# Split layer-norm statistics, a later GpSimd start, and store waits moved to the next use of the buffer

## What is computed

```
x = x + gcn(layernorm(x))            # 512 -> 128, aggregate over edges, 128 -> 512
x = x + alu(layernorm(x))            # small 3-layer net; adds only into columns 128..160
x = x + gnn3(layernorm(x))           # three 512x512 layers, each aggregated over edges
x = x + fff(layernorm(x))            # 16 experts, one per token, 512 -> 2048 -> 512
```

## Time and profile before

| | |
|---|---|
| median of 3 runs | 576.83 us |
| profiled execution | 578.86 us |
| its span | 577.1 us |
| TensorE matmul busy | 526.0 us (91%) |
| VectorE / ScalarE / GpSimd busy | 188.4 / 143.6 / 73.1 us |
| bytes moved by DMA | 145.84 MB, mean 253 GB/s |
| chain that ended last | PE 68%, DMA 16%, DVE 8%, issue 3% |

### The profile page before, as it was taken

The page is one execution under the profiler, slowest core; times in us unless marked ns, Lnnn a source line. Parts: engine busy times, 40 slices in busy tenths (PEclk is TensorE's granted clock), DMA queues, the critical chain, the costliest instruction groups (busy, mean ns, idle before and its releaser), DMA issues.

```text
span 577.1 us, 10036 instructions
## 1 busy us (share of the span) xinstructions
PE 526.0 (91%) x3215; PEld 286.8 (50%) x3215; DVE 188.4 (33%) x566; ACT 143.6 (25%) x504; POOL 73.1 (13%) x99
## 2 busy tenths in 40 slices
PE   1969999989999999999999599999999999978884
PEld 1536667544457466445455245555544364434332
DVE  5998999644410110256730100111111011100110
ACT  1547666112102011003122112222222042202211
POOL 4000000090000000000002222211211212122011
PEclk9979999979999999999999799999999999999998
DMA  6159930001120010027799999999999999999980
GB/s 128 14 174 429 429 133 19 18 1 53 39 73 2 0 73 0 7 86 229 288 389 418 413 396 424 420 424 423 422 423 419 419 430 412 421 416 433 420 371 21
DMA packets 26513, 145.84 MB, mean 253 GB/s; under 512 B 10479, under 2 KB 12729, under 8 KB 16882
## 3 DMA queue, kind: packets, MB, share of 16 engines
q1 hardware_dynamic: 23282, 142.92, 61.4%
q0 software_dynamic: 3200, 2.50, 2.1%
HBM read 142.38 MB, written 4.72 MB: 255 GB/s over the span
## 4 chain that ended last, share of the span: by engine, by line
PE 68%; DMA 16%; DVE 8%; issue 3%; ACT 2%; DVEq 1%; ACTq 1%; POOL 0%; POOLq 0%; SPq 0%
PE P L1168 14%; PE P L1082 13%; DMA w<-in_L_ffn_W 12%; PE P L955 9%; PE P L965 7%; PE P L789 6%; PE P L974 4%; DMA XT<-normed_rows,C 2%; PE P L1133 2%; DMA out<-XT,C 2%; DVE stats L1317 2%; DVE H L1292 1%; PE P L790 1%; PE P L1146 1%; PE P L869 1%
## 5 line engine op out<-in xcount | busy, mean ns | idle before, releaser
L1168 PE MATMUL P<-w,FB 128*64 128x256 f32 x1024 | 115.9, 383 | 2.2 <-DMA w<-in_L_ffn_W 2.2
L1082 PE MATMUL P<-w,H 128*64 128x512 f32 x448 | 100.0, 595 | 9.3 <-DMA w<-in_L_ffn_W 8.8
L1168 PEld LDWEIGHTS P<-w,FB 128*64 128x64 f32 x1024 | 72.1, 138 | 40.6 <-issue 6.6
L718 ACT ACTIVATE FB<-P,FB 128x64 f32<-128x64 f32 x256 | 54.4, 361 | 121.8 <-PE P L1133 121.8
L1575 DVE COPY H<-P 128x512 f32<-128x512 f32 x30 | 20.7, 692 | 195.5 <-PE P L1082 195.0
L789 PE MATMUL P<-H 125*126 125x500 bf16 x176 | 59.0, 414 | 8.1 <-DVE H L1292 4.7
L1082 PEld LDWEIGHTS P<-w,H 128*64 128x64 f32 x448 | 32.1, 137 | 68.7 <-issue 59.3
L1292 DVE TENSOR_SCALAR H<-iota,small 125x626 bf16<-125x626 f16 x176 | 56.6, 382 | 8.7 <-issue 6.9
L619 ACT ACTIVATE H<-G,small 125x126 bf16<-125x126 f16 x132 | 44.2, 392 | 35.3 <-PE P L790 21.8
L955 PE MATMUL P<-G,XT 128*125 128x512 f32 x120 | 52.0, 592 | 0.0
L965 PE MATMUL P<-C,H 125*128 125x313 f32 (+1 forms) x160 | 42.4, 425 | 0.0
(11 more groups left out here) (315 smaller groups left out, 441.8 us busy)
## 6 DMA issues: line engine op xcount, KB each, us to landing
w<-in_L_ffn_W SPq DMA_DIRECT2D x53, 2048.0 KB, 24.8
w<-in_L_ffn_W SPq DMA_DIRECT2D x14, 1024.0 KB, 9.6
G<-in_L_gnn_W SPq DMA_DIRECT2D x3, 1024.0 KB, 5.3
G<-in_L_ffn_W SPq DMA_DIRECT2D x2, 1024.0 KB, 8.3
C<-in_L_ffn_W SPq DMA_DIRECT2D x2, 1024.0 KB, 9.4
xs<-in_L_ffn_W SPq DMA_DIRECT2D x2, 1024.0 KB, 10.2
xn<-in_L_ffn_W SPq DMA_DIRECT2D x2, 1024.0 KB, 10.3
xs<-in_x SPq DMA_DIRECT2D x1, 1120.0 KB
```

What stands on the lines that cost most here:

```text
L718: g = nc.scalar.activation(hT[:, m, :], P[:, 3 + rd, c * SA:(c + 1) * SA], ACT.Gelu, bias=bT[b][:, m:m + 1])
L1082: mm = nc.tensor.matmul(P[g * SA:(g + 1) * SA, h, :], xT[b][:, k, :], w1a[k][:, h, g], start=(k == 0), stop=(k == KD - 1))
L1168: mm = nc.tensor.matmul(P[g * SA:(g + 1) * SA, 7, 0:256], hT[:, m, :], w2_sb[b][:, m, g * 256:(g + 1) * 256], start=False, stop=(m == MH - 1))
```

## The change

Statistics: `bn_stats` of columns 162 to 511 (`CHANGED` = 162) is done while layer 2 of the four-case network runs, into the second half of a new statistics tile `stats2`; after the additions only columns 0 to 161 are left, and `bn_aggr` joins the two parts. To free VectorE, both halves of layer 2's output are now copied by ScalarE. GpSimd waits for `s_feat` beside `s_ahead` before it starts. One `keep_warm` matmul is added ahead of the wait for `s_fTc`, and one is taken from the seven ahead of the norm. Stores: the scatter of tile i waits for the scatter of tile i - 2 just ahead of its own row numbers, and `s_yfree` is raised there; the first pass of the loop is written out, as it has nothing to wait for.

```diff
--- before.py
+++ after.py
@@ -54,6 +54,7 @@
 NF = 5
 RESULT = 100
 FCOLS = 108
+CHANGED = 162
 
 NE, HID = 16, 2048
 MH = HID // 128
@@ -155,6 +156,8 @@
         win_tail = G[:, 1024 + CASES * GE:1024 + CASES * (GE + GT)].rearrange("p (c o) -> p c o", c=CASES)
         fT = G[:, 0:N_NODES]
         y3T = H[:, 2 * N_NODES:3 * N_NODES]
+
+        stats2 = H[:, 2000:2000 + NCH * 12].rearrange("p (c s v) -> p c s v", c=NCH, s=2)
 
 
         feat = FB[0:NC, 0:NCH * GT].rearrange("p (c f) -> p c f", c=NCH)
@@ -500,6 +503,7 @@
             nc.gpsimd.memset(feat, 0.0).then_inc(s_fz, 1)
 
             pool.wait_ge(s_ahead, 1)
+            pool.wait_ge(s_feat, 1)
             for c in range(NCH):
                 nc.gpsimd.tensor_scalar(xn[0:NC, c, FCOLS:DIM], xs[0:NC, c, FCOLS:DIM], mv[0:NC, c, 0:1], rstd[0:NC, c:c + 1],
                                         ALU.subtract, ALU.mult).then_inc(s_ln, 1)
@@ -508,7 +512,7 @@
 
             pool.wait_ge(s_gh, NCH * 3)
             nc.gpsimd.memset(b2_rows, 0.0).then_inc(s_b2z, 1)
-            pool.sem_inc(s_yfree, 2)
+
             def hold(sem, value):
 
                 pool.wait_ge(sem, value)
@@ -525,8 +529,12 @@
                                              in_offset=bass.IndirectOffsetOnAxis(ap=row_in, axis=0),
                                              bounds_check=2 * N_NODES - 1, oob_is_err=False).then_inc(s_xr, 16)
 
-            def scatter(i, b, count):
-
+            def scatter(p, b, count):
+
+                i = 2 * p + b
+                if not (isinstance(p, int) and p == 0):
+                    hold(s_yst[b], 16 * p)
+                pool.sem_inc(s_yfree, 1)
                 pick(row_out[b], 0, i, count)
                 hold(s_ycp, i + 2)
                 nc.gpsimd.indirect_dma_start(out=out.rearrange("t (g n) -> (t g) n", g=2),
@@ -555,16 +563,15 @@
                 i = 2 * p + b
                 hold(s_xT, i + 2)
                 gather(i + 2, 2 * i + 3)
-                scatter(i, b, 2 * i + 4)
+                scatter(p, b, 2 * i + 4)
                 if isinstance(p, int) and i == LARGE:
                     pool.wait_ge(s_ycpB, 1)
                     nc.gpsimd.indirect_dma_start(out=out.rearrange("t (g n) -> (t g) n", g=4),
                                                  out_offset=bass.IndirectOffsetOnAxis(ap=row_outB, axis=0), in_=y_sbB, in_offset=None,
                                                  bounds_check=4 * N_NODES - 1, oob_is_err=False, compute_op=ALU.add).then_inc(s_ystB, 16)
-                hold(s_yst[b], 16 * p + 16)
-                pool.sem_inc(s_yfree, 1)
-
-            with pool.Fori(0, LARGE // 2) as p:
+            for b in range(2):
+                move_rows(0, b)
+            with pool.Fori(1, LARGE // 2) as p:
                 for b in range(2):
                     move_rows(p, b)
             for b in range(2):
@@ -573,7 +580,7 @@
                 for b in range(2):
                     move_rows(p, b)
             for b in range(2):
-                scatter(2 * last + b, b, 4 * last + 3 + b)
+                scatter(last, b, 4 * last + 3 + b)
             for b in range(2):
                 hold(s_yst[b], 16 * last + 16)
             pool.wait_ge(s_ystB, 16)
@@ -675,8 +682,9 @@
                 nc.scalar.activation(ffn_features(layer, t)[:, a:b], P[:, g % 8, 0:b - a], ACT.Relu,
                                      bias=(bf_c[:, t:t + 1] if layer else 0.0)).then_inc(s_fa, 1)
 
-            act.wait_ge(s_y3, 2)
-            nc.scalar.activation(y3T[:, HALF:N_NODES], P[:, 5, 0:N_NODES - HALF], ACT.Identity, bias=b3_c[:, 0:1]).then_inc(s_y3c, 1)
+            for h, (a, b) in enumerate(HALVES):
+                act.wait_ge(s_y3, h + 1)
+                nc.scalar.activation(y3T[:, a:b], P[:, 4 + h, 0:b - a], ACT.Identity, bias=b3_c[:, 0:1]).then_inc(s_y3c, 1)
             sqrt_var()
             copy_transposed()
 
@@ -883,6 +891,7 @@
                     t = nc.tensor.matmul(P[g * GT:(g + 1) * GT, c // 4, (c % 4) * NC:(c % 4 + 1) * NC], feat[:, c, :],
                                          ident[0:NC, 0:NC], start=True, stop=True)
             t.then_inc(s_fT, 1)
+            keep_warm(1, C[0:NC, 0, 0:DIM])
             pe.wait_ge(s_fTc, 1)
             pe.wait_ge(s_win, 16 * 20)
             pe.wait_ge(s_wint, 1)
@@ -938,7 +947,7 @@
             t.then_inc(s_y3, 1)
 
 
-            keep_warm(7, C[0:NC, 0, 0:DIM])
+            keep_warm(6, C[0:NC, 0, 0:DIM])
             ln_no[0] += 1
             transpose_norm()
 
@@ -1307,17 +1316,17 @@
 
             batch_no = [0]
 
-            def norm(chunk_ready=None, batches=ALL_CHUNKS, ahead=0):
+            def norm(chunk_ready=None, batches=ALL_CHUNKS, ahead=0, halves=False):
 
 
                 for first, end in batches:
                     for c in range(first, end):
                         if chunk_ready:
                             chunk_ready(c)
-                        last = nc.vector.bn_stats(stats[0:NC, c, :], xs[0:NC, c, :])
+                        last = nc.vector.bn_stats(stats2[0:NC, c, 0, :] if halves else stats[0:NC, c, :], xs[0:NC, c, 0:CHANGED if halves else DIM])
                     link(last)
                     for c in range(first, end):
-                        last = nc.vector.bn_aggr(mv[0:NC, c, :], stats[0:NC, c, :])
+                        last = nc.vector.bn_aggr(mv[0:NC, c, :], stats2[0:NC, c].rearrange("p s v -> p (s v)") if halves else stats[0:NC, c, :])
                     link(last)
                     ts(rstd[0:NC, first:end], mv[0:NC, first:end, 1], EPS, None, ALU.add).then_inc(s_var, 1)
                     batch_no[0] += 1
@@ -1387,8 +1396,9 @@
 
             ya, ys, ysel = sv(460, NCH, 4), sv(480, NCH, 4), sv(500, NCH, 4)
             res, oh, car = sv(520, NCH, 2), sv(540, NCH * 2, 16), sv(700, NCH)
-            dve.wait_ge(s_y3, 1)
-            ts(y3T[:, 0:HALF], P[:, 4, 0:HALF], b3_c[:, 0:1], None, ALU.add).then_inc(s_y3c, 1)
+            dve.wait_ge(s_xsum, 1)
+            for c in range(NCH):
+                nc.vector.bn_stats(stats2[0:NC, c, 1, :], xs[0:NC, c, CHANGED:DIM])
             dve.wait_ge(s_y3, 3)
             y3 = P[0:NC, 6, 0:2 * CASES * NCH].rearrange("p (c n) -> p c n", c=NCH)
             tt(ya[0:NC], y3[:, :, 0:4], madd[0:NC, :].unsqueeze(2).to_broadcast([NC, NCH, 4]), ALU.mult)
@@ -1404,10 +1414,9 @@
                     res[0:NC].rearrange("p c s -> p (c s)").unsqueeze(2).to_broadcast([NC, NCH * 2, 16]), ALU.is_equal))
             link(tt(oh[0:NC].rearrange("p (c s) n -> p c (s n)", s=2), oh[0:NC].rearrange("p (c s) n -> p c (s n)", s=2),
                     act2[0:NC, :].unsqueeze(2).to_broadcast([NC, NCH, 32]), ALU.mult))
-            dve.wait_ge(s_xsum, 1)
             tt(xs[0:NC, :, 128:160], xs[0:NC, :, 128:160], oh[0:NC].rearrange("p (c s) n -> p c (s n)", s=2), ALU.add)
             link(tt(xs[0:NC, :, 160:161], xs[0:NC, :, 160:161], car[0:NC, :].unsqueeze(2), ALU.add))
-            norm()
+            norm(halves=True)
 
 
             with dve.Fori(0, 3) as l:
```

## The result

The changed kernel takes 571.49 us (median of six runs, 570.94 to 572.00) against 576.09 for the kernel before in the same comparison (573.65 to 578.91); 4.6 us by the medians and 4.4 by the ratio, 0.9923 (0.9902 to 0.9943). The forecast was 571.0.

The account below looks back on a forecast made before the run. The saturated weight stream was taken as the bound, with gains ahead of it counting in full: 0.65 + 3.1 + 1.7 + 0.8 = 6.25 us, 0.5 less for the median, so 576.83 - 5.8 = 571.0; whole range 567.5 to 574.4.

Parts of the forecast that it names:

- The bound: Expert stage from 330 us on: the saturated weight stream, about 421 GB/s, sets the time, not TensorE.
- a sign that I had named: Expert stage: TensorE's waits on weights grow by about 7 us, those of L1082 several us above 8.8.
- Another sign: Everything ahead of the graph layers: the prediction is wrong if the granted clock is 0.50 anywhere there.
- GpSimd at `s_feat`: Four-case network, ahead of the features: two 20-column VectorE operations drop to 0.17 us each, 0.65 us gained.
- Statistics: Norm behind the four-case network: 162 of 512 columns stay on the path, the rest is hidden, 1.7 us gained.
- `keep_warm` and the clock: Four-case network, layer 0 and the first layer 1 group: the filler keeps the clock up, 3.1 us gained.
- Stores: Expert stage, tile 2: the 6.2 us wait for gathered rows goes, but only 0.8 us is won.
- the thin place: Weight stream over 330 to 342 us: 384 instead of 421 GB/s, priced at 1.05 us.
- (b): Expert stage: TensorE is the bound, so the stall is paid out in full, 7 instead of 0.8, 565; chance 0.06.
- (c): Norm: the hidden statistics aren't hidden, VectorE's 2.4 us stay on the path, 573.4; chance 0.06.
- (d): Weight stream, 330 to 556 us: it loses rate and the kernel is slower, 581 at 403 GB/s; chance 0.05.
- rival (a): Four-case network: clock falls anyway, or median run before never had the low stretch; 3.15 us remain, 573.7; chance 0.15.

Follow-up runs that it names:

- h1: Kernel before with half of the bytes in most expert weight loads, old store waits: 555.24 us, ratio 0.9634.
- s4: Kernel before with only the waits for the stores moved to the buffers' next use: 574.54 us, ratio 0.9979.
- g1: Changed kernel with the gather of tile 3's rows issued ahead of tile 0's scatter: 571.73 us, ratio 0.9926 to the kernel before.
- c0: Changed kernel without the nine keep-warm matmuls ahead of the feature transposes and the one ahead of layer 0: 575.02 us, against 571.68 for the changed kernel beside it.
- s1: Kernel before with only one more keep-warm matmul ahead of the wait for the copied features: 574.96 us, ratio 0.9991.
- l1: Changed kernel without the one keep-warm matmul ahead of the wait for the copied features: 571.43 us, ratio 0.9919 to the kernel before.
- l2: Changed kernel with the waits for the stores as in the kernel before: 571.79 us, ratio 0.9919 to the kernel before.
- s3: Kernel before with the split statistics alone, ScalarE copying both output halves and six keep-warm matmuls instead of seven: 573.12 us, ratio 0.9960.
- a1: The changed kernel measured again, unaltered, on another chip: 571.68 us, ratio 0.9916 to the kernel before.

## Why the prediction came out as it did

- **The bound.** Right: half of the bytes take 21.5 us away (h1), the rate stays at 421 to 422 over 360 to 500 in every trace with all the bytes, and a stall taken out comes back as waiting (s4) or as nothing in the time (g1). But a sign that I had named failed. The waits on weights were to grow by about 7 us, those of L1082 "several us above 8.8"; in the trace of after they are 11.2 against 11.0, and L1091's are 6.0. The stall of 2.5 us that was left, and TensorE's stretches at 1.2 GHz, used up the room. Only s4 and g1, where neither is there, show 16.5 to 16.7. Another sign was worded too widely: the clock is at 1.2 GHz from 31.6 to 38.4 us in the trace of after, but so it is somewhere between 31 and 41 us in every other, before too, far ahead of the change.
- **GpSimd at `s_feat`, 0.65 us.** 0.62 between warm-up and transposes in every trace that has it.
- **Statistics, 1.7 us.** 1.76, in every trace that has it. The hidden part, 350 columns, cost 2.22 us for the 2.4 I worked out and had 1.84 us to spare for 1.5.
- **`keep_warm` and the clock, 3.1 us.** The price was right: 3.2 us between the profiles of before and after from the transposes to the network's result, and 3.0 in c0's trace behind the transposes. Its parts were off a little: layer 0 lost 2.42 us, not 2.54 (I had taken its start and its end from two views), and the first group of layer 1 0.8, not 0.55. That the filler buys it for the median run was the step that failed. I read one profile as the program, with a discount of 0.5 us; it should have been the whole 3.1. That profile, 578.86, was above all six timed runs but one. The filler itself bought nothing that could be measured (s1, l1).
- **Stores, 0.8 us.** Right in mechanism, under-sized: 1.8 us by the traces, some 1.1 of it the thin place I had priced at 1.05 (363 to 392 GB/s over 330 to 342 in the traces with the old waits, 422 to 430 with the new). The median of s4 says 1.3, that of l2 only 0.1 to 0.4. The gather was late by 2.5 us with a scatter just ahead of it, which cost nothing (g1).
- **The sum.** 0.62 + 1.76 + 1.8 = 4.2 us, against 4.6 and 5.1 between the medians of two comparisons (4.4 and 4.8 by the ratios). What is over may be the time that the kernel before takes longer in runs of lower clock, as in s3's median; that isn't shown. From the median of six runs the terms give 576.09 - 4.2 = 571.9. I came to 571.0 with a clock term that is mostly absent, stores that were 1.0 too small, and a median of before (576.83) that was 0.7 above the one of six runs. That the forecast came within 0.5 us of the 571.49 is luck in part: two errors of opposite sign, of which the larger was on the clock. My rival (a) named it ("or the median run before never had the low stretch") and put 573.7 beside it; with the stores' true size that is 572.7.
- **Rivals (b), (c), (d).** None came: the stall wasn't paid out, the hidden statistics had cover, and the stream's rate was 421 after the change, and 422 in s4 and g1, where TensorE waits for it most.

## What to carry to other kernels

In a stage that a saturated stream of loads bounds, a compute stall inside it is worth little more than the bytes that the stream failed to move because of it (here 1.1 of 1.8 us, for a stall of 6.2); look for the slice in which the rate dips, and price that. A clock that falls in one profile is an event of that execution until a second one shows it: before paying for it in a forecast, compare another trace, or count only what idle time of the program makes certain.

## What the runs showed of the hardware

- TensorE's clock, with the same instructions up to there and the same gaps (1.42 and 1.47 us busy of 3.25), fell to 1.2 GHz in one trace (before) and stayed at 2.4 GHz in another (s3); in c0, where TensorE was idle from 110.3 to 118.1, it was at 1.2 GHz from about 114 to about 128.
- Layer 0, which keeps TensorE busy all the time, ran through at 1.2 GHz; the clock was back at 128.09.
- In the expert stage the clock fell to 1.2 GHz in every wait of 5.5 to 6.2 us for gathered rows (six traces), in or soon after those of 2.5, 2.3 and 3.2 us in after, a1 and c0, and not after one of 2.5 us in l1.
- A scatter of 128 rows of 1 KB with an add landed in 12.1 us beside 422 GB/s and in 5.0 beside 141; one issued 2.3 us behind a gather took 9.3 us beside 403 GB/s and 8.6 beside 365.
- A gather of the same size issued 2.7 us behind a scatter took 10.6 us; with none ahead of it, at most 8.3 (g1), and 6.2 after a scatter had landed.
- A 20-column VectorE operation beside GpSimd's 404-column ones took 0.48 to 0.51 us, alone 0.16 to 0.17.
